# Sixteen-bit probabilities and values, masks on TensorE and a later output projection in the layers of a fused attention and transformer kernel

## The chip, the cores and the metric

The kernel runs on one core of a Trainium2 chip. The metric is device time in microseconds (us) of one execution; each time given for a run is one such execution, and a comparison uses the median of several. The engines are PE (TensorE: matmuls, with PEld for its weight loads), DVE (VectorE), ACT (ScalarE), POOL (GpSimd) and SP, which issues the DMAs.

## The reference

The input x has 16 sequences of 512 rows by 256 columns, in float32. The result is x + A(xn) + F(xn), with xn the layer norm of x. A is full attention with 16 heads of width 16. F is two transformer layers, each with local attention and a gated feed-forward part; only F's part of the program changes. One layer of F, cut to what matters:

```python
h = shift_token(x)                       # second half of the columns comes from the row before
q, k, v = split(h @ wqkv, 3)             # 8 heads of width 64
q, k = rotary_xpos(l2norm(q) * qs, l2norm(k) * ksc)
# windows of 128 rows; each query window sees its own keys and those of the window before
sim = einsum('bhwid,bhwjd->bhwij', bq * 8, bk)
sim = where((i < j) | (i > j + 128) | (j == -1), -max, sim)
o = einsum('bhwij,bhwjd->bhwid', softmax(sim), bv)
x = x + o @ wo
h = (shift_token(x) - mean) / sqrt(var + 1e-5) * lg + lb
a, g = split(h @ w1 + b1, 2)             # 682 columns each
x = x + (a * gelu(g)) @ w2 + b2
```

## The kernel before, in words

The program has two phases, one after the other. The first (full attention, names m_*) is not touched. The second (names f_*) runs the two layers, each over the 16 sequences. A sequence passes through stages in a software pipeline: in one round, stage A works on sequence i (transposed input XT, query and key projection QK, norms RN and NM, splitting into two float16 parts HI, SH, SQ), stage C on sequence i-1 (values V, transposed queries and keys ST, first scores L1 for the row maximum, transposed maxima LM, second scores L2 and their exponential, probabilities times values PV, transposed output OT, output projection WO), stage N on i-2 (layer norm LN, its transpose XH), and stage F on i-3 (W1, gelu, H1, W2). "C.L2,1" is step L2 of stage C for the second pair of heads; the four pairs are 0 to 3. 13 rounds of a layer run in a loop; before and after them stand shorter sections in which some stages are missing.

The order of the steps on each engine is written out by hand, one list per engine (the table `order`). An engine works through its list strictly in turn, and waits on semaphores. PSUM is four buffers p0 to p3 of 128x1024 float32; a rule (`PsumPlan`) gives each tile the buffer that was taken longest ago. Nearly every product is made of three float16 matmuls (high times high, low times high, high times low part), so that float32 accuracy stays.

In the attention of stage C, L2 makes transposed scores, ACT takes the exponential of each head into a float32 buffer Pl (four buffers, 128x896; a head is 896 columns), POOL sets the masked entries to zero with two affine selects a head, and PE multiplies Pl with the values vl (float32, 64 columns and one of ones for the sum). Those are 14 products a pair of heads, and each float32 product is two matmul instructions on the engine. DVE then divides by the sums (on). OT and WO of the same sequence follow in the same round, so the round ends in PV, OT, WO. WO is followed on DVE by x1 = projection + residual, on which the layer norm of the next round depends.

The lines that matter:

```python
1104  pe.matmul(psum[PV], Pl[h % 4][:, at * W:(at + 1) * W], vl[:, j, h, :], ...)        # float32
1229  act.activation(Pl[h % 4][:], psum[L2][:, 0:NK], ACT.Exp, scale=1 / KBOOST)
1502  pool.affine_select(out=own, in_=own, compare_op=ALU.is_ge, fill=0.0, ...)           # and L1504 for nxt
1354  dve.tensor_tensor(klt[t], u[t] (keys), khh[t] (keys' high part), ALU.subtract)      # step SH
1488  pool.tensor_tensor(q_lo(t), u[t] (queries), q_hi(t), ALU.subtract)                  # step SQ
```

## Time and profile before

| what | us |
|---|---|
| median of 3 runs (3971.88 to 3972.2) | 3972.04 |
| the profiled execution's own time | 3974.68 |
| its span in the profile | 3972.9 |
| PE busy in the span | 3510.6 (88%) |
| DVE busy | 2638.4 (66%) |
| ACT busy | 2148.6 (54%) |
| POOL busy | 1522.5 (38%) |

The page gives each engine's busy time and its share of the span. A matmul's duration in the records is longer than the step to the next one, since matmuls overlap in the engine; how fast PE works is read from the starts of successive rows, not from durations. The layers take the last 2800 us of the span or so.

### The profile page before, as it was taken

How to read it: one execution, taken by the hardware profiler on the slowest of the kernel's cores; microseconds unless marked ns; L12 is line 12 of the kernel's file. 1: busy time of each engine (PE TensorE's matmuls, PEld its weight loads, DVE VectorE, ACT ScalarE, POOL GpSimd, SP SyncE). 2: the span in 40 equal slices, each digit the busy share in tenths (PEclk: the TensorE clock that was granted, in tenths of full speed). 3: DMA queues.
4: the chain of work that ended last, by engine and by line, in shares of the span. 5: the costliest groups of instructions: out<-in, count | busy, mean ns of one | idle time of the engine just before them, and what ended most of it. 6: DMA issues, size and time to landing. Idle time of an engine off the chain costs nothing.

```text
span 3972.9 us, 72434 instructions
## 1 busy us (share of the span) xinstructions
PE 3510.6 (88%) x26976; PEld 2099.6 (53%) x26976; DVE 2638.4 (66%) x4180; ACT 2148.6 (54%) x2585; POOL 1522.5 (38%) x1584
## 2 busy tenths in 40 slices
PE   2888888888866799999999999887999999999999
PEld 1223232323224566667666766555666766667666
DVE  4778777777744567666676666656677666776664
ACT  0566565656543356555555555443655556555554
POOL 1212121111114345455455554343455544455443
PEclk7999999999987899999999999998999999999999
DMA  2222222222120000010000101010000110001101
GB/s 56 48 60 54 58 55 57 56 56 57 45 82 6 14 21 19 18 34 19 21 18 18 34 19 42 20 50 19 27 24 24 34 35 25 24 27 31 37 19 35
DMA packets 149003, 139.02 MB, mean 35 GB/s; under 512 B 11132, under 2 KB 147376, under 8 KB 148912
## 3 DMA queue, kind: packets, MB, share of 16 engines
q1 hardware_dynamic: 148912, 137.78, 13.1%
q8 instruction: 61, 1.00, 0.1%
q14 instruction: 30, 0.25, 0.0%
HBM read 70.40 MB, written 33.55 MB: 26 GB/s over the span
## 4 chain that ended last, share of the span: by engine, by line
issue 29%; POOL 21%; PE 15%; DVE 4%; ACT 2%; POOLq 0%; DMA 0%; SPq 0%; DVEq 0%; ACTq 0%
POOL f_u L1478 7%; POOL f_u L1483 5%; PE f_p L1104 3%; PE f_p L1123 3%; POOL f_hT L1494 3%; POOL f_Pl L1502 2%; PE f_p L1145 2%; PE f_p L1023 2%; POOL f_xb L1511 2%; PE f_p L1086 2%; POOL f_Pl L1504 1%; POOL f_qst L1488 1%; PE f_p L1090 1%; POOL f_mark_l L1499 1%; DVE f_negm L1360 1%
## 5 line engine op out<-in xcount | busy, mean ns | idle before, releaser
L654 DVE TENSOR_REDUCE m_negm<-m_p 128x2 f16<-128x1024 f32 x512 | 608.3, 1221 | 170.4 <-PE m_p L473 168.5
L576 ACT ACTIVATE m_Pr<-m_p 128x1024 f32<-128x1024 f32 x512 | 500.6, 1020 | 163.9 <-PE m_p L492 159.4
L1478 POOL TENSOR_TENSOR f_u<-f_u,f_bt 128x1024 f32<-128x1024 f32 x128 | 301.9, 2358 | 561.2 <-DVE f_bt L1332 561.2
L1104 PE MATMUL f_p<-f_vl,f_Pl 128*128 128x65 f32 x3584 | 426.1, 279 | 30.7 <-POOL f_Pl L1504 30.7
L1104 PEld LDWEIGHTS f_p<-f_vl,f_Pl 128*128 128x128 f32 x3584 | 416.0, 195 | 41.0 <-POOL f_Pl L1504 31.4
L1229 ACT ACTIVATE f_Pl<-f_p 128x896 f32<-128x896 f32 x256 | 220.5, 914 | 328.8 <-PE f_p L1090 221.6
L1494 POOL TENSOR_TENSOR f_hT<-f_gates,f_hT 128x512 f16<-128x512 f32 x192 | 223.8, 1166 | 396.5 <-ACT f_gates L1252 395.1
L501 PE MATMUL m_o<-m_Pr,m_vm 128*32 128x512 f32 x2048 | 341.6, 645 | 13.0 <-ACT m_Pr L576 13.0
L1023 PE MATMUL f_p<-f_wq_h,f_xT_h 128*128 128x512 f16 x768 | 295.8, 385 | 62.4 <-DVE f_mark_x L1318 45.1
L1244 ACT ACTIVATE f_gates<-f_p,f_bias 128x512 f32<-128x512 f32 x192 | 131.4, 684 | 344.8 <-PE f_p L1145 344.7
L1360 DVE TENSOR_REDUCE f_negm<-f_p 128x4 bf16<-128x1024 f32 x256 | 295.7, 1222 | 15.0 <-PE f_p L1056 15.0
L1145 PE MATMUL f_p<-f_xhT_h,f_w_h 128*128 128x512 f16 (+1 forms) x768 | 293.2, 382 | 9.5 <-DVE f_gates L1435 3.8
L1023 PE MATMUL f_p<-f_wq_l,f_xT_h 128*128 128x512 f16 x768 | 294.4, 383 | 0.0
L1023 PE MATMUL f_p<-f_wq_h,f_xT_l 128*128 128x512 f16 x768 | 294.0, 383 | 0.0
L1145 PE MATMUL f_p<-f_xhT_h,f_w_l 128*128 128x512 f16 (+1 forms) x768 | 292.3, 381 | 0.0
L1145 PE MATMUL f_p<-f_xhT_l,f_w_h 128*128 128x512 f16 (+1 forms) x768 | 292.1, 380 | 0.0
L1483 POOL TENSOR_TENSOR f_u<-f_u,f_rn 128x1024 f32<-128x1024 f32 x128 | 243.1, 1899 | 109.5 <-DVE f_mark_v L1350 109.5
L1123 PE MATMUL f_p<-f_w_h,f_hT 128*128 128x256 f16 x1536 | 262.0, 273 | 2.2 <-POOL f_hT L1494 2.2
L473 PE MATMUL m_p<-m_KT,m_QT 48*128 48x512 f16 x1024 | 192.3, 398 | 80.6 <-DMA m_KT<-m_lo 31.4
L1323 DVE TENSOR_REDUCE f_ss<-f_sq 128x16 f32<-128x1024 f32 x128 | 156.0, 1219 | 151.7 <-ACT f_sq L1193 151.7
L492 PE MATMUL m_p<-m_QT,m_KT 49*128 49x512 f16 x1024 | 192.2, 391 | 61.7 <-DVE m_negm L654 35.6
L1371 DVE RECIPROCAL f_rden<-f_p 128x8 f32<-128x8 f32 x128 | 26.5, 207 | 322.2 <-PE f_p L1104 322.2
(219 smaller groups left out, 7533.7 us busy)
## 6 DMA issues: line engine op xcount, KB each, us to landing
f_xs<-out SPq DMA_DIRECT2D x32, 512.0 KB, 4.8
f_xr<-out SPq DMA_DIRECT2D x32, 512.0 KB, 4.6
out<-f_xb SPq DMA_DIRECT2D x32, 512.0 KB, 3.3
m_xin<-in_L_attn_x SPq DMA_DIRECT2D x16, 512.0 KB, 4.1
out<-m_xn SPq DMA_DIRECT2D x16, 512.0 KB, 3.0
m_QT<-m_hi SPq DMA_DIRECT2D x128, 64.0 KB
m_KT<-m_hi SPq DMA_DIRECT2D x128, 64.0 KB
m_xr<-in_L_attn_x SPq DMA_DIRECT2D x16, 512.0 KB, 4.8
```

The lines of the kernel that those rows point to most:

```text
L501: mm = pe.matmul(psum[w.slot("MV", g)][j * VW:(j + 1) * VW, :], vm[I.par][:, kt, g * HG + j, :], Pr[kt % 2][:, j, :], start=(kt == 0), sto ...
L576: act.activation(Pr[kt % 2][:, 2 * u:2 * u + 2, :].rearrange("p h t -> p (h t)"), psum[w.slot("M2", g, kt, u)][:, :], ACT.Exp).then_inc(*w ...
L654: dve.tensor_reduce(negm[:, t, pr // 2, :, pr % 2], psum[w.slot("M1", h, u)][:, :].rearrange("p (a k) -> p a k", a=2), AX.X, ALU.max, nega ...
L1023: mm = pe.matmul(psum[w.slot(key, t)][:, i * INNER:(i + 1) * INNER], a_[:, c, at], b_[:, c, n0:n0 + INNER], start=(c == 0 and k == 0), sto ...
L1104: mm = pe.matmul(psum[w.slot("PV", hp)][:, e * T + t * (DH + 1):e * T + (t + 1) * (DH + 1)], Pl[h % 4][:, at * W:(at + 1) * W], vl[:, j, h ...
L1123: mm = pe.matmul(psum[w.slot(key)][:, t * D:(t + 1) * D], a_[:, c, t * P:(t + 1) * P], b_[:, c, :], start=(c == 0 and k == 0 and t % 2 == ...
L1145: mm = pe.matmul(psum[w.slot("W1", f)][0:rows(f), g * T:(g + 1) * T], a_[:, c, hidden(g, f)], b_[:, c, :], start=(c == 0 and k == 0), stop ...
L1229: act.activation(Pl[h % 4][:], psum[w.slot("L2", h)][:, 0:NK], ACT.Exp, scale=1 / KBOOST)\
L1360: dve.tensor_reduce(negm[:, :, h], psum[w.slot("L1", h)][:, :].rearrange("p (n k) -> p n k", n=NT), AX.X, ALU.max, negate=True).then_inc(* ...
L1478: pool.tensor_tensor(u[t][:], u[t][:], bt[:], ALU.add).then_inc(*bt_used.up(I))
L1483: pool.tensor_tensor(u[t][:].rearrange("p (h d) -> p h d", d=DH), u[t][:].rearrange("p (h d) -> p h d", d=DH), rn[:, t, :].unsqueeze(2).to ...
L1494: pool.tensor_tensor(hT_l[0:n, f, :], hp_[f % 2][0:n, :], hT_h[0:n, f, :], ALU.subtract).then_inc(*hl_ready.up(I))
```

## The change

1. Probabilities in two float16 parts. ACT writes the exponential to one of now two float32 buffers Pl and then copies it to float16 (new step PH, into Pp[h % 4][:, 0]); DVE subtracts that copy from Pl and writes the rest in float16 (new step PL). The exponential of head h waits until PL has read head h-2.
2. Values in two float16 parts: after ACT's copy, DVE subtracts it from PSUM (new step V on DVE, four a round). PV becomes three float16 matmuls a product, of 65, 64 and 65 columns, each with its own weight load.
3. The masks of the second scores are added by PE in L2 (identity times the mask tile, 4 matmuls a head), and POOL's two selects and a mark a head go.
4. OT and WO move to a new stage D, one round later: transposes behind the first ST of the round, projection between the first scores. x1 is then made early in the round that also holds its layer norm.
5. The 42-column rest of the hidden layer: value and gate columns are put side by side in one weight tile, so that W1,5 takes 6 matmuls and not 12.
6. All lists are rearranged. H1 gets three buffers; in the second layer the sum of the residual (ZB) moves on DVE from the round's end to ahead of W2; the roots (rsqrt inside RN and LN) stay on DVE; the load and the conversion of wo move.

The lists, before and after:

```diff
-        "PE": """C.V,0 C.V,1 C.V,2 C.V,3 A.XT C.ST,0 A.QK,0 C.ST,1 A.QK,1 C.ST,2 A.QK,2 C.ST,3 A.QK,3 F.W1,0 F.W1,1 C.L1,0 C.L1,1
-               F.W1,2 C.L1,2 C.L1,3 F.W1,3 F.W1,4 F.W1,5 C.LM F.W2,0 C.L2,0 F.W2,1 F.W2,2 C.L2,1 C.PV,0 C.L2,2 C.L2,3 C.PV,1 C.PV,2
-               C.OT,0 C.PV,3 N.XH C.OT,1 C.WO,0 C.WO,1 C.WO,2 C.WO,3""",
+        "PE": """C.V,0 C.V,1 C.V,2 C.V,3 A.XT C.ST,0 D.OT,0 D.OT,1 A.QK,0 C.ST,1 A.QK,1 C.ST,2 A.QK,2 C.ST,3 A.QK,3 D.WO,0 C.L1,0
+               D.WO,1 D.WO,2 D.WO,3 C.L1,1 C.L1,2 F.W1,0 F.W1,1 C.L1,3 F.W1,2 F.W1,3 C.LM F.W1,4 F.W1,5 C.L2,0 F.W2,0 C.L2,1 F.W2,1
+               F.W2,2 C.L2,2 C.PV,0 C.L2,3 C.PV,1 C.PV,2 N.XH C.PV,3""",
...
+        "ACT": """C.V,0 C.V,1 C.V,2 C.V,3 A.XT C.ST,0 D.OT,0 D.OT,1 A.QK,0 C.ST,1 A.QK,1 C.ST,2 A.QK,2 C.ST,3 A.QK,3 F.W1,0 F.W1,1
+               F.H1,0 F.W1,2 F.H1,1 F.W1,3 C.LM F.H1,2 F.W1,4 F.H1,3 F.W1,5 F.H1,4 C.L2,0 F.H1,5 C.PH,0 A.HI,0 C.L2,1 C.PH,1 C.L2,2
+               C.PH,2 A.HI,1 C.L2,3 C.PH,3 N.XH A.HI,2 A.HI,3""",
...
+        "DVE": """C.V,0 C.V,1 C.V,2 C.V,3 A.XT D.OT,0 D.OT,1 A.QK,0 A.QK,1 D.WO,0 D.WO,1 D.WO,2 A.QK,2 A.QK,3 C.L1,0 D.WO,3 C.L1,1
+               C.L1,2 F.W1,0 F.W1,1 C.L1,3 C.LM A.RN F.W1,2 F.W1,3 F.W1,4 F.W1,5 F.ZB F.W2,0 F.W2,1 N.LN C.PL,0 F.W2,2 C.PL,1 A.SH,0
+               C.PV,0 C.PL,2 C.PL,3 N.XH C.PV,1 C.PV,2 C.PV,3 A.SH,1 A.SH,2  A.SH,3""",
+        "POOL": """A.QK,0 A.QK,1 A.QK,2 A.QK,3 F.H1,0 A.NM,0 F.H1,1 F.H1,2 F.H1,3 F.H1,4 F.H1,5 A.SQ,0 A.NM,1 N.LS A.SQ,1 A.NM,2 A.SQ,2
+               A.NM,3 A.SQ,3""",
+        "SP": """A.XT F.W2,0 N.LX F.W2,1 F.W2,2 C.XR N.XH""",
```

The new and changed steps:

```diff
@@ PE, l2
+                for e in range(2):
+                    for j in range(NT):
+                        pe.matmul(dst(e, j), identb[:], masks[:].rearrange("p a k -> p (a k)")[:, 0:min(2 * W, T - j * W)],
+                                  start=False, stop=False, skip_group_check=True)
@@ PE, pv
-                pe.wait_ge(*masked.at(I, 2 * (2 * hp + 2)))
+                pe.wait_ge(*p_lo_ready.at(I, 2 * hp + 2))
...
-                            mm = pe.matmul(psum[w.slot("PV", hp)][:, e * T + t * (DH + 1):e * T + (t + 1) * (DH + 1)],
-                                           Pl[h % 4][:, at * W:(at + 1) * W], vl[:, j, h, :], start=(t == 0), stop=(j == t),
-                                           skip_group_check=True)
+                            pe.matmul(dst, p_hi, vl[:, j, h, 0:DH + 1], start=(t == 0), stop=False, skip_group_check=True)
+                            pe.matmul(dst[:, 0:DH], p_hi, vl[:, j, h, DH + 1:], start=False, stop=False, skip_group_check=True)
+                            mm = pe.matmul(dst, p_lo, vl[:, j, h, 0:DH + 1], start=False, stop=(j == t), skip_group_check=True)
@@ ACT, l2 and p_hi
+                for h in (2 * hp, 2 * hp + 1):
+                    act.wait_ge(*w.is_full("L2", h))
+                    if h >= 2:
+                        act.wait_ge(*p_lo_ready.at(I, h - 1))
+                    act.activation(Pl[h % 2][:], psum[w.slot("L2", h)][:, 0:NK], ACT.Exp, scale=1 / KBOOST)\
+                        .then_inc(*w.frees("L2", h))
+            def p_hi(I, hp):
                 if hp >= 2:
                     act.wait_ge(*w.is_full("PV", hp - 2))
                 for h in (2 * hp, 2 * hp + 1):
+                    act.wait_ge(*w.is_drained("L2", h))
+                    act.activation(Pp[h % 4][:, 0, :], Pl[h % 2][:], ACT.Copy).then_inc(*p_hi_ready.up(I))
@@ DVE
+            def v_(I, t):
+                dve.wait_ge(*v_hi_ready.at(I, t + 1))
+                dve.scalar_tensor_tensor(vl[:, t, :, DH + 1:], psum[w.slot("V", t)][:, 0:INNER].rearrange("p (h d) -> p h d", h=H),
+                                         1 / WSCALE, vl[:, t, :, 0:DH], ALU.mult, ALU.subtract).then_inc(*w.frees("V", t))
+            def p_lo(I, hp):
+                for h in (2 * hp, 2 * hp + 1):
+                    dve.wait_ge(*p_hi_ready.at(I, h + 1))
+                    dve.tensor_tensor(Pp[h % 4][:, 1, :], Pl[h % 2][:], Pp[h % 4][:, 0, :], ALU.subtract).then_inc(*p_lo_ready.up(I))
@@ PE, w1_
+                if f == NF - 1:
+                    for c in range(NC):
+                        for k, (a_, b_) in enumerate(((wt_h, xhT_h), (wt_l, xhT_h), (wt_h, xhT_l))):
+                            mm = pe.matmul(psum[w.slot("W1", f)][0:HALF + TAIL, 0:T], a_[:, c, :], b_[:, c, :],
+                                           start=(c == 0 and k == 0), stop=(c == NC - 1 and k == 2))
@@ POOL, l2: gone
-                    pool.tensor_tensor(mark_l[:, h:h + 1], mark_p[:], mark_p[:], ALU.add)
-                    pool.affine_select(out=own, in_=own, compare_op=ALU.is_ge, fill=0.0, base=0, ...
-                    pool.affine_select(out=nxt, in_=nxt, compare_op=ALU.is_ge, fill=0.0, base=0, ...
```

How it moves on DVE behind the layer norm, in a round of the loop. Before, the last piece of the layer norm (f_xh), the sum behind W2 (f_xb), the key's low part (f_klt) and the first two divisions of PV (f_rden, f_on):

```order
L1420 TENSOR_SCALAR f_xh<-f_x1s,f_mv,f_rstd 128x128
L1441 REGISTER_ALU
L1445 REGISTER_ALU
L1446 SCALAR_TENSOR_TENSOR f_xb<-f_p,f_xb 128x1024
L1354 TENSOR_TENSOR f_klt<-f_u,f_khh 128x512
L1368 REGISTER_ALU
L1371 RECIPROCAL f_rden<-f_p 128x8
L1372 ISA
L1373 TENSOR_TENSOR f_on<-f_p,f_rden 128x2x4x64
```

And now, in the same place; L1373 is now step PL, the low part of the probabilities (f_Ph from f_Pl):

```order
L1459 TENSOR_SCALAR f_xh<-f_x1s,f_mv,f_rstd 128x128
L1372 ISA
L1373 TENSOR_TENSOR f_Ph<-f_Pl,f_Ph 128x896
L1372 REGISTER_ALU
L1373 TENSOR_TENSOR f_Ph<-f_Pl,f_Ph 128x896
L1481 REGISTER_ALU
L1486 SCALAR_TENSOR_TENSOR f_xb<-f_p,f_xb 128x1024
L1372 REGISTER_ALU
L1373 TENSOR_TENSOR f_Ph<-f_Pl,f_Ph 128x896
L1372 REGISTER_ALU
L1373 TENSOR_TENSOR f_Ph<-f_Pl,f_Ph 128x896
L1390 TENSOR_TENSOR f_klt<-f_u,f_khh 128x512
```

The low parts of the first two pairs of heads stand directly behind the layer norm, and everything that PV needs passes through this list.

On PE, at the start of a round, where the input is transposed (f_xs) and the first queries and keys are projected. Before:

```order
L1005 MATMUL f_p<-f_identf,f_xs 128x128 x8
L1034 ISA
L1035 REGISTER_ALU
L1040 MATMUL f_p<-f_ident,f_qst 128x128 x8
L1040 MATMUL f_p<-f_ident,f_khh 128x128 x8
L1035 REGISTER_ALU
L1040 MATMUL f_p<-f_ident,f_klt 128x128 x4
L1013 REGISTER_ALU
L1023 MATMUL f_p<-f_wq_h,f_xT_h 128x512
```

And now, with the transposes of the attention's output of the sequence before (f_on) between them:

```order
L1007 MATMUL f_p<-f_identf,f_xs 128x128 x8
L1036 ISA
L1042 MATMUL f_p<-f_ident,f_qst 128x128 x8
L1042 MATMUL f_p<-f_ident,f_khh 128x128 x8
L1037 REGISTER_ALU
L1042 MATMUL f_p<-f_ident,f_klt 128x128 x4
L1118 ISA
L1119 REGISTER_ALU
L1122 MATMUL f_p<-f_identf,f_on 128x128 x8
L1118 REGISTER_ALU
L1119 REGISTER_ALU
L1122 MATMUL f_p<-f_identf,f_on 128x128 x8
```

Sixteen transposes that stood near the round's end now stand between the transpose of the input and the first projection that needs it, which comes next.

## Rows read from the trace of the kernel before

**Rows 1.** Busy time by engine in four rounds: PE, PEld, DVE, ACT, POOL, clock, DMA.

```profile
1727.70:2055.10 327.40, 316.26 (x2610) 217.62 (x2609) 218.99 (x392) 186.60 (x232) 166.18 (x172) 1.00 0.07 22
```

**Rows 2.** Instructions of the transposed input: min/median/max ns, first and last start.

```profile
L1005 PE MATMUL f_p<-f_identf,f_xs x256: 272/273/448, 1172.7 to 3766.2; 128*128 128x128 f32 x128
```

**Rows 3.** PE's waits in those four rounds: total us, times, longest.

```profile
PE f_p L1023 <- DVE f_mark_x L1318: 5.4, 4, 1.4
PE f_p L1049 <- DVE f_gates L1435: 2.4, 8, 0.3
PE f_p L1082 <- DVE f_gates L1435: 1.6, 4, 0.4
```

**Rows 4.** PE in order of time: start, us, line, names, shape, count.

```profile
1727.70 1.04 PE L1005 MATMUL f_p<-f_identf,f_xs 128*128 128x128 f32 x8
...
2010.34 0.40 PE L1145 MATMUL f_p<-f_xhT_h,f_w_h 128*42 128x512 f16 x1
...
2012.73 0.38 PE L1145 MATMUL f_p<-f_xhT_l,f_w_h 128*42 128x512 f16 x1
...
2023.49 0.39 PE L1082 MATMUL f_p<-f_mT,f_sel 32*128 32x256 bf16 x8
2023.82 0.94 PE L1086 MATMUL f_p<-f_qkt 128*128 128x256 f16 x8
2024.69 0.56 PE L1090 MATMUL f_p<-f_qkt 64*128 64x256 f16 x8
2025.18 3.34 PE L1104 MATMUL f_p<-f_vl,f_Pl 128*128 128x65 f32 x28
2028.45 0.39 PE L1082 MATMUL f_p<-f_mT,f_sel 32*128 32x256 bf16 x8
...
2055.08 1.04 PE L1005 MATMUL f_p<-f_identf,f_xs 128*128 128x128 f32 x8
2055.95 0.61 PE L1040 MATMUL f_p<-f_ident,f_qst 128*128 128x128 f16 x8
2056.40 0.61 PE L1040 MATMUL f_p<-f_ident,f_khh 128*128 128x128 f16 x8
```

**Rows 5.** DVE's groups in those rounds: count, busy us, mean ns, idle before.

```profile
L1435 DVE SCALAR_TENSOR_TENSOR f_gates<-f_p,f_bias,f_gates 128x512 f32<-128x512 f32 x20 | 14.6, 747 | 3.2 <-ACT f_gates L1244 3.1
L1378 DVE TENSOR_TENSOR f_oT_l<-f_p,f_oT_h 128x1024 f16<-128x1024 f32 x8 | 9.8, 1224 | 4.1 <-ACT f_oT_h L1234 4.0
```

**Rows 6.** ACT's groups, the same view.

```profile
L1229 ACT ACTIVATE f_Pl<-f_p 128x896 f32<-128x896 f32 x32 | 27.6, 914 | 38.4 <-PE f_p L1090 25.1 <-PE f_p L1104 13.3
L1207 ACT ACTIVATE f_khh<-f_u 128x1024 f16<-128x1024 f32 x16 | 16.7, 1044 | 0.0
```

**Rows 7.** POOL's groups, the same view.

```profile
L1488 POOL TENSOR_TENSOR f_qst<-f_u,f_qst 128x512 f16<-128x512 f32 x16 | 20.6, 1289 | 19.6 <-ACT f_khh L1207 19.6
L1502 POOL TENSOR_SCALAR_AFFINE_SELECT f_Pl<-f_Pl 128x512 f32<-128x512 f32 x32 | 20.0, 625 | 0.0
L1504 POOL TENSOR_SCALAR_AFFINE_SELECT f_Pl<-f_Pl 128x384 f32<-128x384 f32 x32 | 17.7, 553 | 0.0
```

**Rows 8.** DVE's low part of the keys beside POOL's of the queries, in time.

```profile
1805.51 0.69 DVE L1354 TENSOR_TENSOR f_klt<-f_u,f_khh 128x512 f16<-128x512 f32 x1
1806.12 2.25 DVE L1354 TENSOR_TENSOR f_klt<-f_u,f_khh 128x512 f16<-128x512 f32 x2
1806.13 1.68 POOL L1488 TENSOR_TENSOR f_qst<-f_u,f_qst 128x512 f16<-128x512 f32 x1 [1.69 <-ACT f_khh L1207]
```

**Rows 9.** DVE in order of time: start and end of one layer norm.

```profile
1852.64 0.28 DVE L1409 BATCH_NORM_STATS2 f_stats<-f_x 128x6 f32<-128x128 f32 x1
...
1855.74 1.02 DVE L248 TENSOR_TENSOR f_tmp<-f_rstd 128x4 f32<-128x4 f32 x1
1856.79 0.16 DVE L249 SCALAR_TENSOR_TENSOR f_tmp<-f_tmp,f_var 128x4 f32<-128x4 f32 x1
...
1862.07 1.20 DVE L1446 SCALAR_TENSOR_TENSOR f_xb<-f_p,f_xb 128x1024 f32<-128x1024 f32 x1
```

More of the change, by code:

```diff
@@ L829, in layers_phase @@
     K = [Inst(f"K{layer}", 0, (lambda i, layer=layer: layer)) for layer in range(L)]
[L830 removed]
+    sections = [Section("queries", {engine: [("WQ", K[0]), ("WS", K[0])] for engine in ENGINES})]
     for layer in range(L):
         more = layer > 0
[L833 removed]
+        r0 = weave(("first", layer), A=0, **(dict(D=-1, N=-1, F=-2) if more else {}))
         r1 = weave(("second", layer), A=1, C=0, **(dict(F=-1) if more else {}))
[L835 to L839 removed]
+        r2 = weave(("third", layer), A=2, C=1, D=0, N=0)
+        for engine in ("ACT", "DVE"):
+            with_steps(r0, engine, "end" if more else "start", ("WO_", K[layer]))
+        with_steps(r1, "PE", "end", ("WO_", K[layer]))
         with_steps(r1, "SP", "end", ("WE", K[layer]))
```

129 lines of the change are left out of this document (59 added, 70 removed).

## The prediction, made before the changed kernel ran

> **What bounds the kernel now.** I read the busy times of a stretch of whole rounds first, then the rows that tell how long a round is, then PE's own waits, and last the engines in order of time. In four rounds of the loop PE is busy 316 of 327.4 us, DVE 219, ACT 187, POOL 166, at the full granted clock of 1.00, the 2.4 GHz level [rows 1]. The round is the distance between transposes of the input: (2055.08 - 1727.70) / 4 = 81.84 us [rows 4]. There are 256 / 8 = 32 such transposes, from 1172.7 to 3766.2 us [rows 2], so 32 rounds or parts of rounds carry the second phase. PE waits for others only (5.4 + 2.4 + 1.6) / 4 = 2.35 us a round [rows 3], mostly for the low part of the transposed input. So PE's own work sets the time. An edit is worth what it takes from PE, until another chain becomes longer.
>
> **The change on PE, part by part (us a round).**
>
> PV: 4 x (2028.45 - 2025.18) = 13.1 goes [rows 4]. It is replaced by 56 products x 3 = 168 float16 matmuls of 64 or 65 columns with a weight load each. The trace has none of that shape. From above: float16 transposes, 128 columns and a 128x128 weight load each, step at 0.45 / 8 = 56 ns [rows 4]; that gives 9.4. From below: columns alone, at 0.87 us for the eight matmuls of L1086 (six of 256, two of 128 columns, 0.49 ns a column) [rows 4], give 32 ns and 5.4. The eight narrow-row matmuls of L1082 with their eight weight loads take 0.33 us, 41 ns each, for another kind of limit, the issue. I take 40 ns: 6.7, and 0.4 for four handovers. Change -6.0, between -7.3 and -3.3.
>
> Masks in L2: 32 matmuls, as wide as the 32 of L1086, 0.87 us a pair of heads [rows 4]: at most 4 x 0.87 = 3.5, and without the handover inside that figure 3.1. I take +3.2.
>
> W1,5: six matmuls of 512 columns fewer, at (2012.73 - 2010.34) / 11 = 0.217 [rows 4]: -1.3.
>
> OT and WO only move. PE's sum is -6.0 + 3.2 - 1.3 = -4.1 (-5.5 to -1.1), so 77.7 with the old waits and 75.4 with none.
>
> A sentence of the Trainium skill speaks against the first term: TensorE: Matmul & The Clock Gate, section Back-to-back issue gap, gives a sustained 81 ns a matmul at 128 columns in a stream of weight loads and matmuls. By it PV would take 168 x 0.081 = 13.6 and gain nothing; this trace steps at 56 ns where the page has 81, so the row decides here, and the rule stays as a rival with a small chance.
>
> **The change on the other engines.** ACT gets eight copies of 896 columns; a 1024-column copy from SBUF lasts 1.04 and the exponential of 896 columns 0.914 [rows 6], so 0.9 each, +7.3; it had 187 / 4 = 47 of 82. DVE gets eight subtractions of 896 columns (a 1024-column one 1.22 [rows 5], a 512-column one 0.69 [rows 8]: 1.1 each, 8.7) and four of 512 from PSUM (0.75 each at most [rows 5], 3.0): 55 + 11.7 = 66.5. POOL loses 8 x (0.625 + 0.553) = 9.4 and eight marks [rows 7]. No engine is full, but DVE and ACT are now in a chain with PE that was short before (POOL's selects took 1.2 a head).
>
> **The chain, which I take as the new bound.** Follow one round from the first V. Up to the end of W1,5 PE has 72 + 66 matmuls of 512 columns (29.9 at 0.217), 24 float32 transposes at 0.87 / 8 (2.6), 84 float16 ones at 0.056 (4.7), the projection's 48 of 256 columns at 0.109 (5.2), and four L1 of 0.87 + 0.49 (5.4), by the steps of [rows 4]: 47.8. The wait for xT (1.35) is now covered by the sixteen OT transposes, 1.7; I leave 0.5 for buffers that DVE frees late. Sum 48.3.
>
> From there DVE decides. Gelu and product of W1,5, behind H1,3 on ACT: 2.3. The layer norm took 1862.07 - 1852.64 = 9.4, with a 1.02 among operations of 0.16 [rows 9]; with POOL's selects gone from there I expect 7.7. Then PL of heads 0 and 1, 1.1 each, with POOL's SQ between: 3.3 (queued behind them: the sum of W2, PL 1, SH 0, PV 0). Then three times round a loop: exponentials of the next two heads (each must wait until PL has freed one of two buffers), two copies, two subtractions. With 0.9 + 0.9 + 0.9 + 1.1 in series and 0.1 at each of four signals this is 4.2; HI 1 on ACT (1.7, all but 0.6 under waits), SH 0 and PV 0 on DVE, and the port, below, bring it to 4.9: 14.6. PE's last PV, 42 x 0.040 = 1.7, and the next round can start. Sum 2.3 + 7.7 + 3.3 + 14.6 + 1.7 = 29.6. In the meantime PE has four L2 at 0.33 + 0.87 + 0.49 [rows 4] and the masks' 0.8 (10.0), W2 (72 x 0.109 = 7.8), three PV (5.0) and the transpose XH (0.9), 23.7; so it waits 4 to 5 us before the last PV, in pieces of 1 to 3.
>
> Round in layer one: 48.3 + 29.6 = 77.9, a gain of 3.9. In layer two the sum ZB (1.2, as a 1024-column operation of [rows 5]) stands before the layer norm in that chain: 79.1, a gain of 2.7. The sections outside the loops hold the same stages with longer waits; I give them the same gain. 16 x (3.9 + 2.7) = 106; the extra weight tile costs a microsecond a layer, 2. The profiled execution's own time is 3974.7, which is 2.6 above the median of the runs: 3974.7 - 104 = 3870.7, and against the median 3868.
>
> **Two inputs in SBUF.** DVE's subtraction of two SBUF operands takes 0.69 alone, but two of them took 2.25 when POOL's operation of 1.68 fell among them [rows 8]: one lost about 1.0. PL is such an operation, eight times a round, in the stretch where POOL now does SQ, NM and LS. In the sum above I have 0.5 a pair and one whole POOL operation in the first.
>
> **The rivals.**
>
> R1, slower: the port. If every one of the eight PL loses the 1.0 of [rows 8], the chain gets 8.0 where I had 2.7: rounds of 83.2 and 84.4, so 16 x (1.36 + 2.56) = 63 slower, 4035. It turns the sign in layer one when a pair costs over 4.9 + 3.9 / 3 = 6.2. For it: POOL's chain HI, SQ, NM runs just there. Against: POOL is idle half of the time, and lost 9.4 itself. 15 of 100.
>
> R2, faster: the chain hides and PE stays the bound. Then 75.4 a round, 32 x 6.4 = 206 less: 3766. For it: DVE is at 66.5 of 75; the layer norm without POOL at the port might take 6.9, and each pair 4.2. Against: that removes only 0.8 + 2.1, to a round of 75.0 in the first layer, so all must go well. 17 of 100.
>
> R3, slower: narrow matmuls step halfway between 56 ns and the 117 ns of the float32 ones (3.27 / 28 [rows 4]), at 86. PV then takes 14.5 + 0.4, PE's sum is +1.8 + 3.2 - 1.3 = +3.7, less the 2.35 of waits: 83.2 a round, 4015. The 81 ns of the Trainium skill's page named above would end near it. The 56 ns of the transposes speak against it. 4 of 100.
>
> R4, no change: PE's new waits of up to 3 us a piece make the granted clock fall now and then. No row of whole rounds shows it below 1.00. It would eat the gain, near 3970. 4 of 100.
>
> The forecast itself: 60 of 100.
>
> **How the numbers follow.** The predicted time is 3868. Within 0.2% (8 us) is what a measurement of this kernel can't tell from no change. The forecast's own range is 3800 to 3940: 1 us more or less in the layer norm, 0.5 in each pair, and 32 to 56 ns for a narrow matmul, of which only the last PV of a round lies in the chain (0.7). For 8 in 10 I go down to 3770, which takes in nearly all of R2, and up to 3990, which leaves out R1 and R3. Faster is the forecast and R2, less 0.01 for the forecast's upper end: 0.76; the same is R4 and that 0.01: 0.05; slower is R1 and R3: 0.19.
>
> **What would show it.** Right: rounds near 78 and 79; PE busy share lower than the 0.966 of now, waits of PE on DVE's f_Ph before PV and on ACT's f_Pl before L2, 4 to 5 us a round together; PE on mark_x no longer waits; f_Ph at 1.1 to 1.6 us mean; narrow matmuls at 30 to 56 ns. The layer norm from first BN to next operation under 8.5. Wrong: PE waits of under 2 us a round (R2), f_Ph means of 2 us (R1), steps of over 80 ns in PV (R3), a clock below 1.00 inside the loops (R4), or a wait at a place I haven't named, such as the load of the input in layer two, which follows XH on SP's queue.

## The result and the profile after

The changed kernel takes 3985.78 us, median of eight runs (3982.24 to 3987.16), beside 3972.51 of the kernel before in the same session (3971.88 to 3978.55): ratio 1.003, 95% interval 1.0019 to 1.0041. It is slower by 0.3%. The forecast was faster, 3868. None of the rivals' times fits either; what happened is a piece of R1, a piece of R4, and one wait that stood nowhere. (A small table of all runs, with what each one started from, stands behind the last experiment.)

Busy time by round in the changed kernel (columns as in [rows 1]): three successive rounds of layer 1, then one of layer 2.

```profile
1627.74:1707.46 79.72, 73.31 (x735) 49.59 (x734) 64.56 (x113) 52.94 (x65) 34.22 (x19) 1.00 0.08 23
1707.46:1789.70 82.24, 76.17 (x735) 51.29 (x734) 64.94 (x113) 53.15 (x65) 34.20 (x19) 0.96 0.07 22
1789.70:1873.64 83.94, 77.68 (x736) 51.84 (x735) 64.99 (x113) 53.15 (x65) 34.20 (x19) 0.94 0.07 22
3098.85:3181.95 83.10, 74.75 (x717) 49.07 (x715) 67.71 (x112) 52.32 (x65) 32.41 (x19) 0.96 0.09 28
```

Where [rows 1] had four equal rounds at a granted clock of 1.00, rounds of layer 1 now differ: 79.7 us at 1.00, 82.2 at 0.96, 83.9 at 0.94. In layer 2 every round is below 1.00. The last twelve rounds of layer 1 average 81.8 and those of layer 2 83.9, where 77.9 and 79.1 were forecast and 81.8 was before. PE's busy time in the round at full clock is 73.3, which is 5.8 under the 79.1 of [rows 1]: the work did leave PE.

The transposes of the input, as in [rows 2]:

```profile
L1007 PE MATMUL f_p<-f_identf,f_xs x256: 272/273/449, 1173.8 to 3766.9; 128*128 128x128 f32 x128
```

From the first to the last of them it is 2593 us in both kernels; from the last to the end of the span it is 3984.8 - 3766.9 = 217.9 where it was 206.7. So all of the loss of 11 us stands behind the last loop round's start, and before that gains (20 us in the three rounds that fill layer 1's pipeline, 4 in layer 2's) and losses (2 a round in layer 2) cancel. That last stretch is not a cause of its own: with the three steps moved that the experiments find (run e10_zb) it is 3839.9 - 3632.3 = 207.6, within 1 us of before.

PE's waits in four rounds of layer 1 (1627.7 to 1953.4), as in [rows 3], and under them those in five rounds of layer 2:

```profile
PE f_p L1112 <- DVE f_Ph L1373: 13.6, 6, 2.7
PE f_p L1025 <- DVE f_on L1409: 8.7, 4, 2.9
PE f_p L1122 <- DVE f_xT_l L1342: 1.5, 4, 0.4
PE f_p L1051 <- DVE f_x L1428: 1.2, 4, 0.3
```

```profile
PE f_p L1112 <- DVE f_Ph L1373: 17.3, 9, 2.5
PE f_p L1084 <- ACT f_Pl L1244: 11.3, 5, 2.3
PE f_p L1025 <- DVE f_on L1409: 7.8, 5, 1.6
```

That is 25.0 / 4 = 6.3 us a round in layer 1 where 4 to 5 were forecast. The first row is the forecast wait of PV for the subtractions; the wait for mark_x is gone, as forecast. The second row was not forecast: L1025 is V, the first step of the next round, and it waits for the divisions f_on of this one. In layer 2 the waits come to 8.0 a round, with a new one of L2 for the exponentials (f_Pl, 2.25).

PE in order of time, as in [rows 4]: one L2 and PV, then the end of a round.

```profile
1764.67 0.39 PE L1084 MATMUL f_p<-f_mT,f_sel 32*128 32x256 bf16 x8
1764.99 0.94 PE L1087 MATMUL f_p<-f_masks,f_identb 128*128 128x256 bf16 x8
1765.77 0.93 PE L1092 MATMUL f_p<-f_qkt 128*128 128x256 f16 x8
...
1767.12 0.20 PE L1112 MATMUL f_p<-f_vl,f_Ph 128*128 128x65 f16 x1
...
1768.39 0.19 PE L1114 MATMUL f_p<-f_vl,f_Ph 128*128 128x65 f16 x1
...
1776.86 1.95 PE L1007 MATMUL f_p<-f_identf,f_xh 128*128 128x128 f32 x8
...
1780.29 0.20 PE L1114 MATMUL f_p<-f_vl,f_Ph 128*128 128x65 f16 x1
1783.10 0.61 PE L1025 MATMUL f_p<-f_wq_h,f_xT_h 128*128 128x512 f16 x1 [2.61 <-DVE f_on L1409]
...
1785.63 0.57 PE L1025 MATMUL f_p<-f_wq_h,f_xT_h 128*128 128x512 f16 x1
```

A PV is 42 matmuls in (1768.39 - 1767.12) / 41 = 31 ns each; the masks take 0.78 a pair. At the end PE stands still for 2.6 us, and the first six steps of V then take (1785.63 - 1783.10) / 6 = 0.42 us, the 1.2 GHz level, where 0.217 is the step at 2.4 GHz. The eight transposes of f_xh (step XH) at 1776.86 last 1.95, where such a group takes 1.04 in [rows 4]: the clock was already low once before. It fell at 1775.77, during PV,2, which had waited 2.65 for its subtraction.

DVE in the same stretch, in order of time:

```profile
1776.77 2.09 DVE L1373 TENSOR_TENSOR f_Ph<-f_Pl,f_Ph 128x896 f16<-128x896 f32 x2 [1.82 <-ACT f_Ph L1252]
1779.90 1.23 DVE L1465 TENSOR_TENSOR f_xhT_l<-f_p,f_xhT_h 128x1024 f16<-128x1024 f32 x1 [1.03 <-ACT f_xhT_h L1261]
...
1781.29 0.69 DVE L1409 TENSOR_TENSOR f_on<-f_p,f_rden 128x512 f32<-128x512 f32 x1
...
1782.35 0.69 DVE L1409 TENSOR_TENSOR f_on<-f_p,f_rden 128x512 f32<-128x512 f32 x1
```

The two f_on are the divisions PV,1 and PV,2; that of PV,3 follows at 1783.19. PE had started PV,2 at 1775.08, behind PV,1, but DVE's queue holds its division until the subtraction PL,3 and XH's low part are done, and XH's waits for ACT's copy. V,0 needs the buffer p0, which PV,2 had: it starts at 1783.10, 0.06 us behind 1782.35 + 0.69.

This round is one with a low clock. The round before it, at 1.00 throughout, runs alike to some 0.02 us for its first 68 us, the 2.65 before PV,2 included. There the clock falls in this round. Then come ACT's copy behind XH and V,0, first in the round at full clock, then in this one (its V,0 is the row at 1783.10 above):

```profile
1697.78 1.02 ACT L1261 ACTIVATE f_xhT_h<-f_p 128x1024 f16<-128x1024 f32 x1
1702.27 0.39 PE L1025 MATMUL f_p<-f_wq_h,f_xT_h 128*128 128x512 f16 x1 [1.59 <-DVE f_on L1409]
```

```profile
1778.85 1.02 ACT L1261 ACTIVATE f_xhT_h<-f_p 128x1024 f16<-128x1024 f32 x1 [1.26 <-PE f_p L1007]
```

Counted from the starts of the rounds (1627.74 and 1707.46), the copy is 1.4 us later at the lower clock and V,0 1.1 later; V,0 has waited 2.61 instead of 1.59, and V itself is slower. The round is 2.5 us longer. So the handover costs 1.6 a round by itself, and the rest of its wait is the low clock, handed on through XH and the divisions queued behind it.

The subtractions a little earlier, DVE's row above POOL's:

```profile
1769.90 5.05 DVE L1373 TENSOR_TENSOR f_Ph<-f_Pl,f_Ph 128x896 f16<-128x896 f32 x2 [0.34 <-ACT f_Ph L1252]
```

```profile
1769.68 2.36 POOL L1539 TENSOR_TENSOR f_xb<-f_x,f_b 128x1024 f32<-128x1024 f32 x1 [3.62 <-DMA out<-f_xb]
1772.24 1.76 POOL L1527 TENSOR_TENSOR f_qst<-f_u,f_qst 128x512 f16<-128x512 f32 x1 [0.20 <-ACT f_khh L1222]
```

Two subtractions take 5.05 us beside POOL's LS and SQ, and 2.09 without (the pair at 1776.77). The first ends at 1772.99, 0.95 behind LS's end (1769.68 + 2.36), the second at 1774.95, 0.95 behind SQ's: each takes about its own 1.08 from the end of POOL's operation. Over the program:

```profile
L1373 DVE TENSOR_TENSOR f_Ph<-f_Pl,f_Ph 128x896 f16<-128x896 f32 x256 | 336.2, 1352 | 101.5 <-ACT f_Ph L1252 101.4
```

The mean of 1.35 lies in the forecast's 1.1 to 1.6; it hides that nearly all of the excess falls on two heads a round, which are in the chain: in layer 1 heads 4 and 5 (means 2.94 and 2.14 over twelve rounds), in layer 2 heads 4 and 6 (2.27 and 1.87); six others are at 1.08 to 1.17. And the layer norm, as in [rows 9], from its first to the next operation, in layer 1:

```profile
1835.89 0.28 DVE L1448 BATCH_NORM_STATS2 f_stats<-f_x 128x6 f32<-128x128 f32 x1
...
1843.34 1.08 DVE L1373 TENSOR_TENSOR f_Ph<-f_Pl,f_Ph 128x896 f16<-128x896 f32 x1
```

1843.34 - 1835.89 = 7.45; forecast 7.7. In layer 2, where ZB stands ahead of it, it takes 3154.35 - 3144.34 = 10.0, since two of its eight last pieces run beside POOL's SQ and NM (the third row) and last 1.18 and 1.94 where the others last 0.34:

```profile
3151.14 1.18 DVE L1459 TENSOR_SCALAR f_xh<-f_x1s,f_mv,f_rstd 128x128 f32<-128x128 f32 x1
3152.24 1.94 DVE L1459 TENSOR_SCALAR f_xh<-f_x,f_mv,f_rstd 128x128 f32<-128x128 f32 x1
3152.19 1.90 POOL L1522 TENSOR_TENSOR f_u<-f_u,f_rn 128x1024 f32<-128x1024 f32 x1
```

### The profile page after: what moved, and what is told of

It reads as the page before. It is cut to its first block, busy times and chain, and to the rows that moved or that the text cites. A ratio compares the mean times of both kernels' runs of the same rounds, so it can differ in the third digit from the quotient of the medians.

```text
span 3984.8 us, 77535 instructions
## 1 busy us (share of the span) xinstructions
PE 3391.8 (85%) x29600; PEld 1972.7 (50%) x29600; DVE 2979.4 (75%) x4633; ACT 2355.6 (59%) x2813; POOL 1251.3 (31%) x815
## 3 DMA queue, kind: packets, MB, share of 16 engines
q8 instruction: 66, 1.08, 0.1%
## 4 chain that ended last, share of the span: by engine, by line
PE 40%; DVE 17%; issue 6%; ACT 6%; POOL 1%; DMA 1%; DVEq 0%; SPq 0%; ACTq 0%; POOLq 0%
PE f_p L1025 13%; PE f_p L1161 10%; PE f_p L1132 4%; DVE f_Ph L1373 3%; PE f_p L1042 3%; DVE f_negm L1396 2%; PE f_p L1051 2%; DVE f_xh L1459 2%; ACT f_Ph L1252 2%; PE f_p L1087 1%; PE f_p L1007 1%; PE f_p L1092 1%; DVE f_on L1409 1%; DVE f_xT_l L1342 1%; DVE f_ss L1349 1%
## 5 line engine op out<-in xcount | busy, mean ns | idle before, releaser
L1373 DVE TENSOR_TENSOR f_Ph<-f_Pl,f_Ph 128x896 f16<-128x896 f32 x256 | 336.2, 1352 | 101.5 <-ACT f_Ph L1252 101.4
L1025 PE MATMUL f_p<-f_wq_h,f_xT_h 128*128 128x512 f16 x768 | 314.3, 409 | 62.0 <-DVE f_on L1409 50.6
L1025 PE MATMUL f_p<-f_wq_l,f_xT_h 128*128 128x512 f16 x768 | 312.8, 407 | 0.0
L1396 DVE TENSOR_REDUCE f_negm<-f_p 128x4 bf16<-128x1024 f32 x256 | 298.1, 1221 | 17.0 <-PE f_p L1058 16.6
L1025 PE MATMUL f_p<-f_wq_h,f_xT_l 128*128 128x512 f16 x768 | 310.1, 404 | 0.0
L1112 PE MATMUL f_p<-f_vl,f_Ph 128*128 128x65 f16 x1792 | 188.5, 197 | 134.9 <-DVE f_Ph L1373 101.9
L1527 POOL TENSOR_TENSOR f_qst<-f_u,f_qst 128x512 f16<-128x512 f32 x128 | 199.7, 1560 | 272.5 <-ACT f_khh L1222 272.5
L1475 DVE SCALAR_TENSOR_TENSOR f_gates<-f_p,f_bias,f_gates 128x512 f32<-128x512 f32 x192 | 141.6, 749 | 188.8 <-ACT f_gates L1267 184.0
L473 PE MATMUL m_p<-m_KT,m_QT 48*128 48x512 f16 x1024 | 192.8, 399 | 80.2 <-DMA m_KT<-m_lo 31.7
L1112 PEld LDWEIGHTS f_p<-f_vl,f_Ph 128*128 128x128 f16 x1792 | 169.5, 99 | 156.9 <-DVE f_Ph L1373 93.9
L1161 PE MATMUL f_p<-f_xhT_h,f_w_h 128*128 128x512 f16 x640 | 244.2, 382 | 2.4 <-DVE f_mark_h L1467 2.4
L1161 PE MATMUL f_p<-f_xhT_h,f_w_l 128*128 128x512 f16 x640 | 243.6, 381 | 0.0
```

The source lines that it names most:

```text
L1025: mm = pe.matmul(psum[w.slot(key, t)][:, i * INNER:(i + 1) * INNER], a_[:, c, at], b_[:, c, n0:n0 + INNER], start=(c == 0 and k == 0), sto ...
L1112: pe.matmul(dst, p_hi, vl[:, j, h, 0:DH + 1], start=(t == 0), stop=False, skip_group_check=True)
L1161: mm = pe.matmul(psum[w.slot("W1", f)][0:rows(f), g * T:(g + 1) * T], a_[:, c, hidden(g, f)], b_[:, c, :], start=(c == 0 and k == 0), stop ...
L1373: dve.tensor_tensor(Pp[h % 4][:, 1, :], Pl[h % 2][:], Pp[h % 4][:, 0, :], ALU.subtract).then_inc(*p_lo_ready.up(I))
L1396: dve.tensor_reduce(negm[:, :, h], psum[w.slot("L1", h)][:, :].rearrange("p (n k) -> p n k", n=NT), AX.X, ALU.max, negate=True).then_inc(* ...
```

## The experiments

Columns are those of the views above. My theory T1: the divisions hold back the next round's V (the handover). T2: the lower clock costs time of its own. T3: GpSimd's operations at the port lengthen subtractions that are in the chain. The kernel before took 3972.5 to 3977.4 us as the median of its runs in the five sessions, so medians of different sessions compare to within some 5 us.

### e1_div: the divisions earlier

```diff
-C.PV,0 C.PL,2 C.PL,3 N.XH C.PV,1 C.PV,2 C.PV,3
+C.PV,0 C.PL,2 C.PV,1 C.PL,3 C.PV,2 N.XH C.PV,3
```

> Only VectorE's order at the round's end is other: the divisions PV,1 and PV,2 stand before PL,3 and before XH instead of behind both. Theory T1 (handover): the next round's V,0 waits 2.6 to 2.8 us for the buffer that the division PV,2 frees, and then runs at the lower clock (0.43 us a 512-column matmul instead of 0.217, some 12 of them: 2.6). The division PV,1 fits into a gap of VectorE, so V,0 no longer waits: a gain of 2.7 to 4 us a round, 32 x 3 = 96, about 3890 us, and the clock in the loops near 1.00. Rival T2 (the clock falls after the short waits before PV,1 to PV,3): the wait goes, but the clock still falls in each round; gain 1 to 1.5 us a round, 3940 to 3955. Rival T3 (VectorE and GpSimd at the port set the end of PL,3, and VectorE is busy to the end): the wait only moves to V,1 or PV,3: within 15 us of 3986.

Measured 3930.65 (ratio to before 0.9878, 0.9859 to 0.9897): 55 us under the changed kernel. V's wait for f_on is down from 8.7 to 0.8 us in four rounds of layer 1; 1.2 us a round came back as a wait of the transposes XT, which want a buffer that V's low part frees:

```profile
PE f_p L1112 <- DVE f_Ph L1373: 11.9, 6, 2.7
PE f_p L1007 <- DVE f_vl L1367: 4.8, 3, 1.8
```

Rounds are 80.2 and 81.9. T1's wait was real. The gain is less than T1's 96 and the clock still fell once a round in layer 1, as T2 said.

### e3_mask2: the masks twice

```diff
-                for e in range(2):
+                for e in (0, 1, 0, 1):
                     for j in range(NT):
                         pe.matmul(dst(e, j), identb[:], masks[:]...
```

> The mask matmuls of L2 are issued twice (the same mask added two times): 0.78 us more of TensorE for each pair of heads, 3.1 us a round. If TensorE's own work still set the round, it would cost 32 x 3.1 = 100 us: 4085. By the chain through exponential, copy and subtraction (T1), the four L2 lie beside VectorE's layer norm and subtractions, and TensorE waits 6 to 8 us a round there: under 0.7 us a round, 3986 to 4008, or less than nothing if the added work keeps the clock up.

4006.3 (1.0078): +20.5, 0.64 us a round for 3.1 us of added work. TensorE's sum no longer sets the round. The mean hides a difference: rounds of layer 1 grow from 81.8 to 83.3, so there half of the added work shows, and those of layer 2 do not grow (83.9 and 83.7).

### e4_ls: GpSimd's sum LS last

```diff
-A.SQ,0 A.NM,1 N.LS A.SQ,1 A.NM,2 A.SQ,2 A.NM,3 A.SQ,3
+A.SQ,0 A.NM,1 A.SQ,1 A.NM,2 A.SQ,2 A.NM,3 A.SQ,3 N.LS
```

> GpSimd's sum LS (2.36 us, two inputs in SBUF) goes from between NM,1 and SQ,1 to the end of GpSimd's round. T3 (port): the subtraction PL of head 4, 3.09 us beside LS, falls to 1.1 to 1.6; it is in the chain, so a gain of 1.5 to 2 us a round: 3922 to 3938. T1: the end of VectorE's queue before the division PV,2 moves by the same 1.5 to 2, so T1 expects the same as long as nothing else collides; what tells them apart is the wait before V,0, which T1 leaves at 2.6 and T3 shortens. Rival: the collision only moves to the next operation on GpSimd (SQ,1 now beside PL): no change, within 10 us of 3986.

3941.46 (0.9916, 0.9899 to 0.9932): 44 less. The subtractions over the program, from its page:

```profile
L1373 DVE TENSOR_TENSOR f_Ph<-f_Pl,f_Ph 128x896 f16<-128x896 f32 x256 | 283.6, 1148 | 121.3 <-ACT f_Ph L1252 121.3
```

336.2 - 283.6 = 53 us less of DVE. T3's place holds, at 3 us above its range. That the 44 is close to the 53 is in part chance: the loop's rounds are 1.6 us shorter in layer 1 and only 0.6 in layer 2, and some 8 us come from the three rounds that fill layer 2's pipeline. V,0 still waits 4.9 / 5 = 1.0 a round, where it was 8.7 / 4 = 2.2.

### e7_both: e1_div and e4_ls together

> e1_div and e4_ls together. Alone they gave 55 and 44 us against the changed kernel. If they are two places in one chain whose gains add (T1 and T3 separate): 3985.8 - 99 = 3887. If both only shorten the stretch from PL of head 4 to the division PV,2, so that the second finds TensorE not waiting: about 3925.

3884.25 (0.9768, 0.9754 to 0.9781): the gains add (55 + 44 = 99, measured 101). They are two places.

### e5_otback: OT and WO back in their round

```diff
-C.PV,1 C.PV,2 N.XH C.PV,3
+C.PV,1 C.PV,2 C.OT,0 N.XH C.PV,3 C.OT,1 C.WO,0 C.WO,1 C.WO,2 C.WO,3
```

(and out of their places in the later round, on ScalarE and VectorE too; the divisions stand as in e1_div).

> The attention's transposes OT and the projection WO are back in the round that made them, at its end (with the divisions in the order of e1). T1: WO covers the freeing of the buffers, so V,0 doesn't wait; but OT,1 waits for the division PV,3 (0.9) and WO,2 for the two parts of it (about 1.5), at a low clock afterwards, 2.5 to 3 us a round more than e1, and the end sections lose the 11 us that the changed kernel has more there: 3890 + 32 x 2.7 - 11 = 3965. Rival: moving the projection is itself what costs (its work in the later round delays something there): then this is at or under e1.

4218.38 (1.0615): a miss by 250. The largest wait is not at OT at all:

```profile
PE f_p L1051 <- DVE f_negm L1396: 18.4, 4, 4.6
```

L1051 is L1, which waits 4.6 us a round for the maxima: the changed order had the projection between the L1 steps as cover. So the move of WO is worth much by what it covers there; I had credited it with 0.5 and the mark_x wait. This run cannot tell what V,0's wait would be with WO at the end and L1's order repaired.

### e6_fill and e11_fill5: PE's wait before PV,2 filled

```diff
                 pe.wait_ge(*w.is_free("PV", hp))
+                for _ in range(10 if hp == 2 else 0):
+                    pe.matmul(psum[w.slot("PV", hp)][:, 0:T], identb[:], mT[:], start=True, stop=True, ...)
                 pe.wait_ge(*p_lo_ready.at(I, 2 * hp + 2))
```

(e11_fill5, on e7_both; e6_fill has 20 of 256 columns from masks, on e1_div.)

> e1_div, and TensorE fills its wait before PV,2 (2.65 us in e1_div, for VectorE's subtraction of head 5) with 20 float16 matmuls of 256 columns into the tile that PV,2 overwrites: 2.2 us, nothing else is other. Theory T2 (the clock): in e1_div the granted clock falls to 0.5 at 68.9 us of a round of layer 1, right behind that wait, for 3.4 us, and the transposes XH take 1.95 where 1.04 would do and PV,3 steps at 55 ns where 31 would do. With the wait filled the clock stays at 1.00 in layer 1 and XH and PV,3 lose nothing: 0.5 to 1.5 us a round less in layer 1, up to as much in layer 2: 3930.7 - (12 to 40) = 3890 to 3918. Rival: the fall comes from elsewhere in the round, or TensorE's lower clock stands beside VectorE's chain, which goes on as before: within 10 us of e1_div, or some us slower by the filler.

3995.65 (1.0046): 65 more than e1_div. In layer 1 V,0 stood still each round, for 4.2 to 4.6 us, with no releaser in the trace:

```profile
PE f_p L1025 <- issue: 17.9, 5, 4.6
```

Layer 2 shows no such row; there the clock rose from 0.96 to 0.99 and rounds stayed at 82.0 beside 81.9.

> e7_both, and TensorE's wait before PV,2 is filled with 10 matmuls of 512 columns (2.2 us) into the tile that PV,2 overwrites: the time of e6_fill's filler in half as many instructions. In e7_both the layer-1 rounds in which the granted clock stays at 1.00 take 76.5 us, those with one 3.4 us stretch at 0.5 take 77.9. T2 (the clock): all rounds of layer 1 become 76.5 and some of layer 2's fall stretches go: 10 to 25 us less, 3860 to 3875. In e6_fill TensorE then stood still for 3.7 us in front of V,0 in layer 1 alone, with nothing that released it: if that comes from the number of instructions in the loop, it is absent or shorter here with half of them; if it comes from the filled wait itself, it is here too: 3940 or more.

3907.05 (0.9821): 23 more than e7_both. The row "issue" is absent. That speaks for the number of added instructions as what brings the stall, and not the time they fill, but the two runs differ in their base and in the filler's tile too; what the stall is stays open. A round of layer 1 of e11_fill5, and two of e7_both:

```profile
1773.07:1851.51 78.44, 75.52 (x746) 50.40 (x746) 63.76 (x113) 52.57 (x66) 33.16 (x20) 1.00 0.08 23
```

```profile
1764.33:1842.26 77.93, 74.59 (x736) 50.26 (x735) 62.60 (x112) 52.78 (x66) 32.79 (x20) 0.98 0.08 24
1920.29:1996.82 76.53, 73.17 (x736) 49.40 (x735) 61.86 (x112) 52.58 (x66) 31.22 (x20) 1.00 0.08 24
```

With the clock held at 1.00 every round of layer 1 is 78.4, not 76.5. But this run did not fill a wait. In e7_both PE goes through PV,1 and PV,2 without a pause, and its one long wait in a round of layer 1 stands before PV,3, at 69.8 us:

```profile
1679.35 0.20 PE L1112 MATMUL f_p<-f_vl,f_Ph 128*128 128x65 f16 x1 [2.65 <-DVE f_Ph L1373]
```

The filler before PV,2 was added work in front of XH: XH starts at 68.3 us of the round instead of 66.1, ScalarE's copies HI behind it come later, and with them SH,3 and V's low part, for which XT now waits 1.7. So the 23 us are the filler's own price, and this run says nothing against T2. The rounds of e7_both do test it. In the two shown above and in the two below, the one with a low clock is the longer by 1.4; the two below (they start at 1531.59 and 1609.53) are alike to 0.02 us on every engine up to 70.8 us, where the clock falls in the first and not in the second. From 71 to 73 us in each:

```profile
1602.59:1604.59 2.00, 2.00 (x14) 0.91 (x12) 1.92 (x6) 0.00 (x0) 2.00 (x2) 0.50 0.00 0
1680.53:1682.53 2.00, 1.99 (x18) 0.88 (x15) 1.92 (x6) 0.00 (x0) 2.00 (x2) 1.00 0.00 0
```

The 24 matmuls of V then take 6.6 us instead of 5.4, and the rounds are 77.9 and 76.5. Nine of twelve rounds of layer 1 are of the longer kind. So T2 holds in the repaired kernel too, at 1.4 us in such a round, 9 x 1.4 = 13 us in layer 1.

### e12_afill: the same filler in the changed kernel

> The changed kernel itself, with TensorE's wait before PV,2 filled by 10 matmuls of 512 columns into the tile that PV,2 overwrites. If the low clock makes the long rounds (T2): the stretches at 0.5 go or shrink to the one behind V,0's wait, rounds of layer 1 fall from 82.0 to 79.7 to 80.5, of layer 2 by about 1: 3986 - (16 x 2 + 16 x 1) = 3938. If the handover and the port make them long and the clock falls beside it (T1, T3): within 15 us of 3986, with the clock higher and V,0 waiting longer instead.

3960.55 (0.9964): 25 less. Here PE does wait before PV,2 in layer 1 (2.65, above), so the filler fills a wait. Three successive rounds of layer 1:

```profile
1704.43:1784.15 79.72, 75.48 (x747) 50.47 (x745) 64.53 (x112) 52.94 (x66) 34.20 (x19) 1.00 0.08 23
1784.15:1864.01 79.86, 75.46 (x747) 50.47 (x745) 64.67 (x112) 52.93 (x66) 34.35 (x19) 1.00 0.08 23
1864.01:1946.76 82.75, 78.42 (x747) 51.26 (x745) 64.80 (x112) 53.17 (x66) 34.27 (x19) 0.96 0.07 22
```

Rounds at 1.00 take 79.7 to 79.9 although PE does 2.2 us more work in them; seven of twelve are at 1.00 where five were. So T2 holds in the changed kernel, and 25 us is a lower bound of what the clock costs it: five of twelve rounds of layer 1 still fall below 1.00, and in layer 2 PE waits before PV,3, so that the filler is added work there. In the changed kernel itself the mean round of layer 1 is 81.8 and one at 1.00 is 79.7, which is 12 x 2.1 = 25 us in layer 1 alone.

### e8_gate and e9_gatezb: GpSimd waits for all subtractions

```diff
-A.SQ,0 A.NM,1 N.LS A.SQ,1 A.NM,2 A.SQ,2 A.NM,3 A.SQ,3
+A.SQ,0 A.NM,1 C.PL,0 A.SQ,1 A.NM,2 A.SQ,2 A.NM,3 A.SQ,3 N.LS
+            def p_lo_done(I, _):
+                pool.wait_ge(*p_lo_ready.at(I, H))
```

> e1_div, and GpSimd waits with its second SQ, NM and all that follows (LS last) until VectorE has done the subtraction of head 7, so that no operation of GpSimd with two inputs in SBUF runs beside PL of heads 2 to 7. T3 (port): the eight f_Ph of a round fall from a mean of about 1.35 us to 1.0 to 1.1 each, PL,3 ends 3 to 3.5 us sooner, and GpSimd's chain still ends before the transposes of the next round want it (it had 15 us to spare at SQ,3): 2.5 to 3.5 us a round less than e1_div, 3820 to 3850, below e7_both. Rival (GpSimd's chain and HI, SH behind it were not off the path): TensorE waits at ST,1 to ST,3 for f_qst or f_klt instead, and the time is at or over that of e7_both.

4003.59 (1.0068). The mean of f_Ph fell to 1.09, the gain did not come:

```profile
PE f_p L1007 <- DVE f_vl L1367: 17.4, 4, 4.4
```

The rival was right, at another place than I named: XT waits for the buffer that V's low parts free, these stand behind SH,3 on DVE, and SH,3 waits for HI,3 behind GpSimd's delayed NM,3.

> e8_gate, and layer 2's sum ZB (1.2 us on VectorE) goes from between W1,5 and the layer norm into a gap behind W1,3, where VectorE idles 1.8 us. If ZB stands in the chain that sets layer 2's round, 16 x 1.2 = 19 us less than e8_gate; if VectorE's queue has slack there, no change (within 5 us).

3961.64 (0.9962): 42 less than e8_gate, over twice the 19.

### e10_zb, e13_azb: ZB off the chain

```diff
-F.W1,2 F.W1,3 F.W1,4 F.W1,5 F.ZB F.W2,0
+F.W1,2 F.W1,3 F.ZB F.W1,4 F.W1,5 F.W2,0
```

> e7_both, and layer 2's sum ZB goes from the place between W1,5 and the layer norm into the gap behind W1,3. With e8_gate the same move gave 42 us, 3.3 a round of layer 2, where the prediction has 1.2 for ZB: it takes the sum off the chain and starts the layer norm and all behind it sooner. If that holds here, layer 2's rounds fall from 81.6 to 78.3, near the 77.6 of layer 1, and the time to 3884 - 52 = 3832. If only ZB's own 1.2 counts: 3884 - 19 = 3865.

3841.72 (0.966, 0.9647 to 0.9673): 43 less than e7_both; layer 2's rounds fall from 81.5 to 78.3. It beats both kernels: 3.4% faster than the one before.

> The changed kernel with the sum ZB of layer 2 moved from before the layer norm to behind W1,3. The prediction's term: ZB costs 1.2 us a round of layer 2, so 3986 - 19 = 3967. By e10_zb, where the same move gave 42: 3944. If the handover at the end of the round hides it: within 8 us of 3986.

3957.49 (0.9956): 28 less in the changed kernel. By the medians ZB costs 1.8 us a round of layer 2 there and 2.7 in e7_both (3.2 in a round of the loop), both over its own 1.2. A wait of L2 for exponentials (f_Pl, the middle row of layer 2 above) goes with it in both. The traces show why: with ZB ahead the layer norm runs into POOL's SQ and NM and takes 10.0 (above); in e10_zb it ends before them, and PL,0 starts at 54.1 us of a round instead of 57.4 in e7_both.

### e14_hi: ScalarE's copies HI later

```diff
-C.PH,2 A.HI,1 C.L2,3 C.PH,3 N.XH A.HI,2 A.HI,3
+C.PH,2 C.L2,3 C.PH,3 A.HI,1 N.XH A.HI,2 A.HI,3
```

> e10_zb, and ScalarE's second pair of copies HI (1.6 us) goes from before the exponentials of heads 6 and 7 to behind their copies. In e10_zb the exponential of head 6 could start at 63.5 us of a round, when the subtraction of head 4 has freed its buffer, but HI holds ScalarE until 64.6. If that sets the end of PL,3: 1 us a round less, 3842 - 32 = 3810. Rival: HI, NM, SQ and SH of the next sequence then end later and the transposes XT wait for V's low parts behind SH,3 (as in e8_gate): 3842 to 3900.

3962.23 (0.9969): 121 more than e10_zb. PE's wait for f_Ph fell to 5.4 / 4 = 1.4 a round, and the one of XT rose to 16.6 / 4 = 4.2, as in e8_gate. The rival was right.

### b1_masks, b2_w15 and e15_w15: single terms of the sum

b1_masks is the kernel before with only the mask matmuls in L2 and without GpSimd's selects. b2_w15 is the kernel before with only W1,5 in six matmuls; e15_w15 is e10_zb with W1,5 in twelve.

> The kernel before with one part of the change alone: the mask matmuls of L2 on TensorE, GpSimd's two selects a head gone. The prediction's term: 3.1 to 3.5 us a round on an engine that sets the round (it waits 2.35 us of 81.8): 3972 + 32 x 3.2 = 4074, 4040 at the least. Rival: GpSimd's selects at the port made the layer norm 9.4 us and others longer, and what is got back there (2 us a round) shortens a chain that sets the round too: 4000 to 4020.

4052.33 (1.0188). A round of it:

```profile
1648.63:1733.52 84.89, 82.12 (x686) 57.15 (x685) 54.60 (x98) 46.63 (x59) 31.32 (x19) 1.00 0.07 22
```

84.9 - 81.8 = 3.1 a round, the term as forecast, at a clock of 1.00 as before. The whole program is 22 under the 4074 expected: the 24 rounds in the middle of the two loops pay 73, all the rest next to nothing.

> The kernel before with another part alone: W1,5's two halves in one group of six matmuls instead of twelve. The prediction's term: 1.3 us a round less on the engine that sets the round: 3972 - 42 = 3930, plus 2 for the extra weight tile. Rival: TensorE only waits longer for the gate's product or for the layer norm behind it: 3965 to 3975.

3972.92 (0.9991, 0.9981 to 1.0): nothing. PE's waits in four rounds, against [rows 3]:

```profile
PE f_p L1024 <- DVE f_mark_x L1333: 5.4, 4, 1.4
PE f_p L1124 <- DVE f_gates L1451: 4.7, 4, 1.2
```

The second row is new: W2 waits 1.2 us for the buffer that W1,5's product frees. The 1.3 turned into a wait, since gelu and product of W1,5 take their time whatever PE does.

> e10_zb with W1,5 in two halves again, twelve matmuls where six do. The prediction's term: 1.3 us a round, 32 x 1.3 = 42 us more: 3884, since the gate's product of W1,5 starts the layer norm and VectorE's chain behind it. Rival (as in the kernel before, where this term was worth 0 to 3 us): within 10 us of 3842.

3875.10 (0.9752): +33, 1.0 a round. In VectorE's chain the term is real.

All runs, with the median, the run that each one started from, and the difference to that run:

| run | started from | us | difference |
|---|---|---|---|
| changed kernel | kernel before | 3985.8 | +13 |
| e1_div | changed kernel | 3930.7 | -55 |
| e3_mask2 | changed kernel | 4006.3 | +21 |
| e4_ls | changed kernel | 3941.5 | -44 |
| e12_afill | changed kernel | 3960.6 | -25 |
| e13_azb | changed kernel | 3957.5 | -28 |
| e5_otback | e1_div | 4218.4 | +288 |
| e6_fill | e1_div | 3995.7 | +65 |
| e7_both | e1_div and e4_ls | 3884.3 | -46 and -57 |
| e8_gate | e1_div, with LS last | 4003.6 | +119 to e7_both |
| e9_gatezb | e8_gate | 3961.6 | -42 |
| e11_fill5 | e7_both | 3907.1 | +23 |
| e10_zb | e7_both | 3841.7 | -43 |
| e14_hi | e10_zb | 3962.2 | +121 |
| e15_w15 | e10_zb | 3875.1 | +33 |
| b1_masks | kernel before | 4052.3 | +75 |
| b2_w15 | kernel before | 3972.9 | -5 |

## Why the prediction was wrong

**PE's terms** were right, and right where I weighed the page. PV's step is 31 ns, the lower bound; I took 40. With it PE's sum is -6.0 - 1.5 + 3.2 - 1.3 = -5.6, and PE's busy time at full clock is 5.8 lower. The rule of the Trainium skill (TensorE: Matmul & The Clock Gate, Back-to-back issue gap), 81 ns a matmul in a stream of weight loads at 128 columns, would have had PV at an estimated 13.6; these matmuls, of 64 and 65 columns, step at 31. R3 is out. The masks cost 0.78 a pair for 0.8.

**VectorE's part of the chain** was right in sum in layer 1, with some luck. From the end of W1,5 on PE I had 2.3 + 7.7 + 3.3 + 14.6 + 1.7 = 29.6. In the trace the layer norm takes 7.45, PL,0 2.1, the three pairs up to the end of PL,3 (1776.77 + 2.09) 15.7, and the last PV 1.4 to 1.6; with 2 for gelu and product that is 28.7. The part before it, from V to the end of W1,5, is 49.4 where I had 48.3. Inside the 28.7 an error of one sign covers one of the other: the port cost 3 us more than two bare subtractions, at one pair (heads 4 and 5, 5.05), where I had 0.5 in each.

**The step that failed** is "PE's last PV, 42 x 0.040 = 1.7, and the next round can start". It could not: V,0 needs a buffer that the division PV,2 frees, and on VectorE's queue that division stood behind PL,3 and XH. Before, OT,1 and four WO (5 us of PE) stood between the last PV and V; the change took that cover away, and I wrote that "OT and WO only move". I listed what each new wait delays, but not which buffer the first step of a round takes. The wait is 1.6 us a round at full clock and 2.6 to 2.9 in the rounds of layer 1 whose clock has fallen just before; e1_div all but removes it and gives 55 us. A round of layer 1 at full clock is then told in full: 49.4 + 28.7 + 1.6 = 79.7, for a forecast of 48.3 + 29.6 = 77.9.

**The clock.** The sum has no term for it: it stands only in R4, with 4 of 100, because no row of whole rounds showed less than 1.00. That row was of a PE that waited in pieces of at most 1.4. Here it fell to 0.5 in seven of twelve rounds of layer 1 and in all of layer 2. The first fall of a round of layer 1 comes 0.4 to 0.7 us behind the end of the wait of 2.6 to 2.7 before PV,2, ahead of V,0's wait, which it makes longer. The same wait stands in the five rounds without a fall, so no run here tells what decides it. The price is 2.1 us a round of layer 1 on average, more than the handover's 1.6 at full clock, and still 1.4 in nine of twelve rounds of e7_both and e10_zb. The forecast had PE waiting in pieces of 1 to 3 us, which was right, and nothing in the sum for what the clock would make of them.

**The port.** R1 said all eight subtractions would lose 1.0. Two of them lost nearly 3 together and the others little, because POOL's LS and SQ fell on heads 4 and 5 alone in layer 1 (in layer 2 heads 4 and 6 lost 2.0 together). The Trainium skill (GPSIMD Engine Reference, Key points) has contention of the two engines for VectorE's instructions with two inputs in SBUF; the 5.05 beside LS and SQ, and 2.09 without, agree. Moving one operation gave 44 us.

**ZB** was priced at its own 1.2 in layer 2, with the layer norm at 7.7 behind it; it costs 1.8 in the changed kernel and 2.7 with the other two repaired, since it pushes the layer norm beside POOL's SQ and NM, where it takes 10.0.

**The end.** I gave the sections outside the loops the loops' gain. Those that fill layer 1's pipeline gained 20 us, those that fill layer 2's 4; the last loop round and the sections that drain layer 2's lost 11.

Together: 3985.8 - 55 (divisions) - 44 (LS) = 3887, and 3884 was measured for the two. ZB's 43 was itself measured from there, so its sum proves nothing more; in the changed kernel alone the same move gave 28. The forecast of 3868 lies near the change with two orders repaired (e7_both, 3884), but partly by luck: its layer 1 has 77.5 where 77.9 was forecast, with the low clock in it that the forecast left out, and its layer 2 has 81.5 where 79.1 was forecast. It was not a forecast of the change as it stood.

Open: what holds V,0 for 4.2 to 4.6 us in e6_fill's layer 1; what decides whether the clock falls behind a wait of 2.65; what the changed kernel would take with the clock held up in every round, since e12_afill holds it in only some; and what e7_both would give with the filler before PV,3, where its wait is.

## What to carry to other kernels

When a change removes work from the end of a loop's body, list the buffers (here the PSUM tiles) that the first steps of the next round take, who frees each, and what that engine's in-order queue holds before it. When a chain through several engines becomes the bound, walk every queue along it for work that isn't part of it (a sum, a division, a copy for the next item): here three moves of single steps, no work removed, were worth 3.6%. When you fill a wait to test the clock, check in the trace of that very kernel that the wait is where the filler goes, and compare rounds of one run with and without a fall before you compare runs. A term of PE's sum is worth its length only where the step behind it waits for it: six matmuls less gave nothing in the kernel before, though PE was busy 97% of it, and twelve in their place cost 33 us in e10_zb.

## What the runs showed of the hardware that I had not expected

- Float16 matmuls of 64 and 65 columns, each with its own 128x128 weight load, step at 31 ns at 2.4 GHz and 55 ns at the 1.2 GHz level (the changed kernel's PV,2, from 1776.04 to 1776.80: 14 steps).
- In e7_both's layer 1 PE has one long wait a round, 2.65 us. It ends at 69.8 us of the round. In nine of twelve rounds the granted clock fell to 0.5 for a time, at 69.3 to 71.2 us, in three it stayed at 1.00; two rounds side by side, one of each kind, are alike to 0.02 us up to the fall. The longer rounds take 77.9, the others 76.5.
- A subtraction of 128x896 with both inputs in SBUF takes 1.08 us alone; two beside GpSimd's LS (2.36) and SQ (1.76) took 5.05, each ending 0.95 behind the end of GpSimd's operation. A 128x128 piece of the layer norm, 0.34 alone, took 1.94 beside GpSimd's NM (1.90).
- With 20 more matmuls in a loop's body PE stood in front of the loop's first matmul for 4.2 to 4.6 us a round in layer 1 and not at all in layer 2 (e6_fill); with 10 of twice the width, on another order of VectorE and GpSimd, it did not (e11_fill5).
